# Products that nobody reads in front of TensorE's waits, in a one-core token, attention and feed-forward tower

## What is computed

```python
def _L0_tok_ref(...):          # tokens -> h, by a table of 28 rows and a 3-wide window
    cont = sliding_window_mean(pca_lookup[ids]) @ proj_w + proj_b
    fused = concatenate([emb[ids], cont]) @ fus_w + fus_b
    return layernorm(fused) * ln_g + ln_b

def _L0_attn_ref(X, Wq, Wv, q_norm_w, v_norm_w):     # 16 heads of 16
    K = X.reshape(B, L, H, d)
    Q = rms_norm_multihead((X @ Wq.T).reshape(B, L, H, d), q_norm_w)
    V = rms_norm_multihead((X @ Wv.T).reshape(B, L, H, d), v_norm_w)
    W = jnp.cumsum(jnp.einsum('blhd,blhe->blhde', K, V), axis=1)
    return jnp.einsum('blhd,blhde->blhe', Q, W).reshape(B, L, D)

def _L0_ffn_ref(x, w1, conv_w, conv_b, w2):          # 8-bit activations, ternary weights
    h = bit_linear(x, w1)
    h = silu(depthwise_conv1d(h, conv_w, conv_b))
    return bit_linear(h, w2)

h = _L0_tok_ref(...)
h = h + _L0_attn_ref(_layernorm(h), ...)
h = h + _L0_ffn_ref(_layernorm(h), ...)
```

## Time and profile before

| | us |
|---|---|
| median of 3 runs | 291.01 (289.68 to 291.11) |
| the profiled execution, its own time | 293.25 |
| its span, from first to last instruction | 291.5 |
| TensorE busy | 200.8 (69%) |
| VectorE busy | 199.6 (68%) |
| ScalarE busy | 159.5 (55%) |
| GpSimd busy | 106.6 (37%) |
| mean granted TensorE clock | 0.80 of full speed |

### The profile page before, as it was taken

One profiled execution on the slowest core, in us unless ns is written; L12 is line 12 of the kernel. 1 busy time (PEld: TensorE's weight loads), 2 busy tenths in 40 slices (PEclk: granted clock), 3 DMA queues, 4 the chain that ended last, 5 costly groups with the idle time before them and its releaser, 6 DMA issues.

```text
span 291.5 us, 4867 instructions
## 1 busy us (share of the span) xinstructions
PE 200.8 (69%) x1456; PEld 147.2 (50%) x1456; DVE 199.6 (68%) x555; ACT 159.5 (55%) x282; POOL 106.6 (37%) x225
## 2 busy tenths in 40 slices
PE   0459377078429969776985997698589767676624
PEld 0126345056328648554854775485467556344312
DVE  2834518945691893898589489858937987785671
ACT  0201050014713795687597668759774975996902
POOL 8102821043105437436424734642513324333300
PEclk9999659559956987996898799689859978665757
DMA  6970010101102012103111220311112024011011
GB/s 152 329 274 2 0 36 9 29 2 36 32 6 62 14 36 38 36 17 57 38 36 39 40 73 15 57 38 36 41 36 74 0 52 48 12 36 37 2 36 36
DMA packets 29403, 14.23 MB, mean 49 GB/s; under 512 B 15616, under 2 KB 28098, under 8 KB 29378
## 3 DMA queue, kind: packets, MB, share of 16 engines
q1 hardware_dynamic: 27888, 13.28, 19.0%
q10 hardware_dynamic: 1490, 0.65, 0.8%
HBM read 5.51 MB, written 2.10 MB: 26 GB/s over the span
## 4 chain that ended last, share of the span: by engine, by line
PE 35%; DVE 27%; issue 11%; ACT 10%; SPq 9%; DMA 7%; DVEq 1%; ACTq 0%
PE PO L750 7%; PE PA L687 6%; SPq L306 5%; DMA feat<-sd 4%; PE PY L791 4%; PE PA L699 3%; SPq L283 3%; PE PH L765 3%; PE PS L709 3%; PE PO L744 3%; ACT w_s L546 2%; ACT tap L540 2%; DVE ST L1069 2%; PE PS L732 2%; DMA mask_b<-in_mask_dram 2%
## 5 line engine op out<-in xcount | busy, mean ns | idle before, releaser
L436 POOL TENSOR_TENSOR hid<-hid,tap 128x508 f32<-128x508 f32 x32 | 40.9, 1282 | 42.3 <-DVE hid L1127 42.3
L765 PE MATMUL PH<-xsT,w1q 128*128 128x256 f16 x256 | 44.8, 306 | 16.0 <-DVE hid L1127 15.9
L537 ACT ACTIVATE hid<-PH,cb_s,cw_x 128x256 f32<-128x256 f32 x64 | 35.9, 561 | 19.6 <-PE PH L765 19.2
L765 PEld LDWEIGHTS PH<-xsT,w1q 128*128 128x128 f16 x256 | 24.4, 105 | 33.4 <-issue 25.3
L732 PE MATMUL PS<-QP,KM 128*128 128x256 f32 x128 | 35.2, 403 | 5.9 <-DVE ST L1069 3.2
L1127 DVE SCALAR_TENSOR_TENSOR hid<-PH,cw_x,hid 128x254 f32<-128x254 f32 x64 | 30.3, 477 | 12.6 <-ACT tap L540 12.2
L546 ACT ACTIVATE w_s<-hid 128x512 f32<-128x512 f32 x32 | 36.0, 1138 | 5.4 <-POOL hid L436 5.3
L750 PE MATMUL PO<-VD,ST 128*64 128x32 f32 x512 | 35.8, 266 | 0.0
L750 PEld LDWEIGHTS PO<-VD,ST 128*64 128x64 f32 x512 | 34.1, 187 | 0.0
L732 PEld LDWEIGHTS PS<-QP,KM 128*128 128x128 f32 x128 | 23.0, 198 | 14.6 <-issue 12.3
L540 ACT ACTIVATE tap<-PH,cw_x 128x256 f32<-128x256 f32 x64 | 29.9, 468 | 0.0
(11 more groups left out here) (186 smaller groups left out, 400.3 us busy)
## 6 DMA issues: line engine op xcount, KB each, us to landing
QP<-QT SPq DMA_DIRECT2D x32, 64.0 KB, 2.1
VD<-Vn SPq DMA_DIRECT2D x32, 64.0 KB, 2.1
out_dram<-y SPq DMA_DIRECT2D x8, 256.0 KB, 2.2
ids_b<-in_ids_dram SPq DMA_DIRECT2D x4, 256.0 KB, 5.7
mask_b<-in_mask_dram SPq DMA_DIRECT2D x4, 256.0 KB, 6.9
w_s<-in_w1T_dram SPq DMA_DIRECT2D x1, 1024.0 KB, 10.0
w_s<-in_w2T_dram SPq DMA_DIRECT2D x1, 1024.0 KB, 12.1
fusw_s<-in_fusw_dram ACTq DMA_DIRECT2D x2, 256.0 KB, 5.2
```

Source lines behind the costliest of these rows:

```text
L436: nc.gpsimd.tensor_tensor(part, part, tap[:, c % 2, :, :, 0:T - 1], ALU.add).then_inc(tap0_ok, 1)
L537: nc.scalar.activation(hid[:, j, :, :].rearrange("p u t -> p (u t)"), hidps(j), ACT.Identity, bias=cb_s[:, j:j + 1], scale=cw_x[:, j, 1:2])
L765: ins = nc.tensor.matmul(hidps(j), w1q[:, k, j * 128:(j + 1) * 128], part[:, s, :, k, :], start=(n == 0), stop=(n == 2 * KC - 1))
```

## The change

One tile of 128 x 256 float16 ones (`warm`) is set by VectorE as its first instruction. A helper `keep_warm(n, bank)` issues n products of it (128 x 128 stationary, 256 columns moving) into a part of PSUM which the next real product overwrites. It is called with n = 24, 12, 12 and 4 in the head, 6 in every `keys_queries`, 16 in `state` for g = 0 and 1, and 10 in `attend` (1,1) of every group. In these three functions the order of the waits is changed too, so that the call stands behind the waits which make the bank free and in front of the others. In all 212 products are added: 52 + 48 + 32 + 80.

```diff
+        warm = sb("warm", [128, UT], F16)
...
+            def keep_warm(n, bank):
+                for _ in range(n):
+                    nc.tensor.matmul(bank, warm[:, 0:128], warm[:, :], start=True, stop=True)
+            pe.wait_ge(warm_ok, 1)
+            keep_warm(24, HB[1][:, 0:UT])
             pe.wait_ge(ld_pf, 32)
...
             ins.then_inc(pf_ps, 1)
+            keep_warm(12, HB[1][:, 0:UT])
             pe.wait_ge(ld_tab, 64)
...
             nc.tensor.matmul(PS[1][32:64, 0:D], pca_s[:, :], pf_s[:, :], start=True, stop=True).then_inc(tab_ps, 1)
+            keep_warm(12, HB[1][:, 0:UT])
             pe.wait_ge(pool_c, 8)
...
             ins.then_inc(tt_ps, 1)
+            keep_warm(4, HB[1][:, 0:UT])
             pe.wait_ge(tct_ok, 1)
...
             def keys_queries(g):
                 if g == 0:
                     wait(pe, tabkq_ok, 2)
-                wait(pe, row_ok[g % 2], 64 * (g // 2 + 1))
                 wait(pe, tn_ok, min(g + 2, NP))
                 free_pa(g - 1)
+                keep_warm(6, PA[:, 0, 0:UT])
+                wait(pe, row_ok[g % 2], 64 * (g // 2 + 1))
...
             def state(g):
+                wait(pe, o1_ok, 2 * g)
+                if g < 2:
+                    keep_warm(16, PO[:, 0:UT])
                 wait(pe, vn_ok, g + 1)
                 wait(pe, x0_ok, g + 1)
-                wait(pe, o1_ok, 2 * g)
...
             def attend(g, u, k):
+                wait(pe, bd_ok, g + 1)
+                if u == 1 and k == 1:
+                    keep_warm(10, PO[:, 0:UT])
                 wait(pe, st_ok[u][k], g + 1)
                 wait(pe, vd_ok[g % 2], 64 * (g // 2 + 1))
-                wait(pe, bd_ok, g + 1)
...
+            nc.vector.memset(warm[:, :], 1.0).then_inc(warm_ok, 1)
             nc.vector.memset(projb_x[:, :, :], 0.0).then_inc(row_c, 1)
```

More of the change, by code:

```diff
@@ L207, in lm_tower_kernel @@
         zero_ok, pool_c, row_c, dve_c = (sem(n) for n in ("zero_ok", "pool_c", "row_c", "dve_c"))
-        sel_c, const_ok = sem("sel_c"), sem("const_ok")
+        sel_c, const_ok, warm_ok = sem("sel_c"), sem("const_ok"), sem("warm_ok")
         f_c, f_ok = sem("f_c"), sem("f_ok")
```

## The result

| | before | after |
|---|---|---|
| median | 292.43 us (20 runs) | 289.32 us (20 runs) |
| ratio | | 0.988, 95% interval 0.985 to 0.991 |
| profiled execution, own time / span | 293.25 / 291.5 us | 287.52 / 285.8 us |
| mean granted clock | 0.80 | 0.885 |

What follows compares the result with a forecast made beforehand. Waits bound the kernel, with TensorE's keys-to-`sum_q` piece on the path and slowed by a falling clock. Terms -7.9 - 1.0 - 2.8 + 0 + 3.7 = -8.0 us off the 291.01 median gave 283.0 us, range 277.6 to 290.

Steps and rivals of the forecast that it cites:

- rival (a): Whole kernel: the clock rises late, so products catch only some turns; -2.8 us, about 288 us; chance 0.2.
- Length times clock: Keys to `sum_q`, turns 2 to 8: 3.15 us at full clock; turns 4 to 8 lose 9.9 us, each reaching the end.
- 7.9 + 1.0: Turns 4 to 8 save 7.9 us by a held or earlier-rising clock; group 7 in turn 9 saves 1.0.
- The 80%: Turns 4 to 8: share of the 9.9 us clock loss expected to be recovered, giving -7.9 us.
- The ten products in turn 4: Before `attend` (1,1), turns 4 to 8: at full clock the delay is hidden by 0.5 us, uncovered 0.1 to 0.6.
- The price of one product: Any added product: 0.115 us at full clock, 0.205 at half; ten cost 1.15 or 2.05 us.
- The head, -2.8: Start of the kernel: products raise the clock from half, shortening float32 products; -2.8 us, bounds -4.0 and 0.
- Turn 1: 0: Six products before keys of group 0 cost +1.2 us, an earlier clock rise saves 1.7 in scores; taken as 0.
- Turns 2 and 3: +3.7: 16 products per turn lie wholly on the path at full-clock price, +1.85 us each turn; bounds +1.5 and +6.5.
- (b): Turns 4 to 8 gain nothing because the clock falls only behind a longer idle gap; 292 us; chance 0.05.
- (c): Keys end 1 us sooner, but ScalarE's passes or VectorE's list end last and swallow gains; 288 to 290 us; chance 0.08.
- (d): Products run at half clock without raising it, keys start 2 us late in turns 4 to 8; 309 us; chance 0.12.

Runs made afterwards that it cites:

- late_only: Changed kernel with only the products in front of keys and attend of groups 2 to 7 kept; 291.85 us against 292.59 for the kernel before, ratio 0.9935.
- no_early: Changed kernel without its products for groups 0 and 1 (keys, state, attend); 285.06 us against 292.59 for the kernel before, ratio 0.965.
- best1: Changed kernel without products for groups 0 and 1 and without the six before keys of group 2; 283.57 us against 292.05 before, ratio 0.975.
- memset_only: Kernel before with only VectorE's memset of the tile added as first instruction; 294.09 us against 294.17, ratio 0.992.
- the third trace: Changed kernel traced again with nothing altered; keys of group 3 to the end took 174.1 us, and the clock fell at 186.8 and 210.7 us.

## Why the prediction was right and where it failed

**The direction was right and the size wrong: 8 us less were forecast, 3.5 measured (4.5 by the mean of the four traces).** That the time still lies in the range is partly luck: the upper bound had been set to take in two rivals, and 289.3 is nearer to rival (a)'s 288 than to the forecast of 283.0. Term by term, with the table of traces above:

- *Length times clock, 3.15 us for the piece, and each us of it a us of the kernel.* Right in its length: six of seven pieces take 3.2 us. Right in its effect from turn 5 on: keys stand 23.3, 23.7 and 23.6 us apart in the trace after, where 23.0 was worked out, and keys 4 to keys 7 are 5.6 us shorter on average of the four. Not in turn 4, where 0.9 was booked and nothing gained. The third stretch, with turn 9, is 8.1 us shorter on average where 7.9 + 1.0 was forecast; 9.3 in the two traces in which the clock held best. The 80% taken for it was about right as a sum.
- *The ten products in turn 4, priced at about nothing.* Not contradicted where the head has its products too. At full clock they take 1.27 us; at half clock, as in `late_only`, `no_early` and `best1`, 2.3 us on the path. But keys 0 to keys 3 take 78.3 us in `best1` and 79.1 on average with the head alone. In `late_only`, without the head, keys 2 to keys 3 take 1.9 us more than without products.
- *The price of one product.* At half clock it was too low: the ten take 2.25 us up to the next product, where 2.05 was worked out, and the six 1.1 to 1.4, where it was 1.2.
- *The head, -2.8.* The start of keys 0 is 2.4 us earlier on average, with 1.4 us of turn 1's six products in it, so the head itself is -3.8 (-3.6 by nine other traces with the head's products and without those six). But the head alone gave back 1.7 us on the way to keys 3, where the row landed 1.1 to 1.6 us late, so 2 of 2.8 were left.
- *Turn 1: 0.* Wrong: +1.4. The six took 1.4 us where 1.2 were priced, and the clock rose at 42.7, 10.4 us behind the start of keys, exactly as far behind it as before (45.1 against 34.70). The scores gained nothing.
- *Turns 2 and 3: +3.7.* **This is the step that failed:** the sum added the full-clock price of the products and nothing else, and so took the shorter piece behind them as gained in full, with no wait at its end. Keys 0 to keys 3 are longer by 6.0 us. The 32 products there take 2.25 + 1.10 and 2.25 + 1.39 = 7.0 us, nearly all at half clock, and the shorter pieces behind them give back 1.35 and 1.56: +4.1, close to the 3.7. What was not in the sum is the rest: the DMAs of the queries start behind keys and take as long as before, so that the shorter piece ends in a wait. In turn 2 the clock falls behind that wait and the scores take 1.3 us more; in turn 3 TensorE waits 0.57 us more for the same DMAs than before. (`memset_only` has no products, but its clock rose early in that piece, and it shows the same wait, 0.58 us: it goes with the shorter piece.) The sum had no such term. `down`, which stands between piece and scores from turn 5 on and covers that transfer, is missing in the turns 2 to 4.

So of the 4.5 us between the forecast of -8.0 and the -3.5 measured, turns 1 to 3 explain 3.7 (1.4 + 2.3), the late part 0.8 on average, the head the other way 1.0; by the four traces the sum is -4.5. The rest, 1 us, is on the side of the comparison: the four traced executions took 289.3 us on average, as the timed ones, but the stretches of the traces without products add up to 292.1 us, 1.4 more than the timed median of 292.43 leaves for a span.

The rivals. (a), the clock that rises late, is partly what happens in executions like the third trace. (b), a clock that falls only behind a long idle gap, so that turns 4 to 8 gain nothing: turn 4 to the end gained 8.1. The falls at 186.8 and at 210.7 stand behind gaps of 1.1 and 1.6 us with work on both sides, and filling a gap of 1.1 us removed the fall at 70 us. The Trainium skill ("TensorE: Matmul & The Clock Gate", section "HAM oscillation") puts the fall behind one long gap; the traces here go against that rule. (c), swallowed gains, came true in the turns 2 and 3, which it had not named, and in turn 4, which it had, though by the late row and not by ScalarE. (d) did not come about: in turn 7 of the third trace, with the six at half clock, the clock rose at 190.3 us, as keys started.

## What to carry to other kernels

In this kernel products that nobody reads were worth their place in front of a wait in which other engines work anyway, and directly ahead of a run of real products on the path; where the wait had already ended, they cost their half-clock price in full (2.25 us for ten), and only the piece behind them paid it back. Before a saved us is booked, look for the next wait behind the shortened piece: a transfer that starts at the piece's head keeps its length, and here the gap it left (1.1 us) took the clock down again. Where the clock is in play, cut several traces of the same kernel at fixed points before believing a difference of one.

## What was not expected of the hardware

- The same kernel with the same code kept the clock at 1.00 from 124.7 to 244.1 us in one execution, and lost it at 186.8 and 210.7 in another; the twenty timed executions of it lie between 286.3 and 293.3 us.
- A gap of 1.1 us between two dense pieces at full clock was followed by a fall to 0.50 (turn 2, four traces of four), and with eight products in it, 1.05 us, the clock stayed up (one trace). In turn 4 a gap of 1.03 us was followed by a fall in the same four traces, and in the kernel before the same gap was not.
- In the head, 24 products of 256 columns from 1.24 us on brought the clock to 1.00 at 5.2 us, after 19 of them; with it up, the float32 products there took half their time.
